# Query-stationary scores, block-diagonal values, a first norm from a channel-major copy of x, and new banks and orders on all engines

## The reference

```python
def _tc_rmsnorm(x, t, gw, gb, bw, bb):
    g = (t @ gw.T + gb)[:, None, :]
    b = (t @ bw.T + bb)[:, None, :]
    inv_rms = jax.lax.rsqrt(jnp.mean(x * x, axis=-1, keepdims=True) + EPS)
    return g * x * inv_rms + b
...
    q, k, v = ((x @ W.T).reshape(B, L, H, dh) for W in (Wq, Wk, Wv))   # 16 heads of 16
    p = jax.nn.softmax(jnp.einsum('blhd,bmhd->bhlm', q, k) / scale, axis=-1)
    o = jnp.einsum('bhlm,bmhd->blhd', p, v).reshape(B, L, D)
    return o @ Wo.T
...
def _swiglu(x, gate_w, hid_w, out_w):
    return jax.nn.silu(x @ gate_w.T) * (x @ hid_w.T) @ out_w.T
x1 = x + _attention(_tc_rmsnorm(x, t, g1w, g1b, b1w, b1b), Wq, Wk, Wv, Wo)
return x + x1 + _swiglu(_tc_rmsnorm(x1, t, g2w, g2b, b2w, b2b), gate_w, hid_w, out_w)
```

## Time and profile before

| | |
|---|---|
| time, median of 3 runs | 991.04 us (990.25 to 996.09) |
| span of the profiled execution | 991.4 us |
| PE / DVE / ACT / POOL busy | 96% / 67% / 57% / 45% |
| share of PE in the chain that ended last | 90% |
| mean granted clock of PE | 0.983 |
| a steady tile, first scores to first scores | about 58.3 us |

### The profile page before, as it was taken

The page is one execution under the profiler, slowest core; times in us unless marked ns, Lnnn a source line. Parts: engine busy times, 40 slices in busy tenths (PEclk is TensorE's granted clock), DMA queues, the critical chain, the costliest instruction groups (busy, mean ns, idle before and its releaser), DMA issues.

```text
span 991.4 us, 24429 instructions
## 1 busy us (share of the span) xinstructions
PE 954.4 (96%) x9112; PEld 817.3 (82%) x9112; DVE 661.2 (67%) x1178; ACT 561.7 (57%) x1271; POOL 447.6 (45%) x393
## 2 busy tenths in 40 slices
PE   6679999999999999999999999999999999999788
PEld 5568888889888898888889888888978888897767
DVE  3856777676777757676675767667576776757552
ACT  6645556565655655565465566646556565655342
POOL 4355345254534535454453545435354552535242
PEclk9688999999999999999999999999999999999999
DMA  5100010000100000010000101000010100000000
GB/s 183 45 1 22 2 38 8 22 21 0 42 0 22 20 21 21 0 42 0 21 21 5 37 0 42 0 21 21 0 42 0 42 0 21 21 0 22 2 22 22
DMA packets 18971, 21.71 MB, mean 22 GB/s; under 512 B 640, under 2 KB 18240, under 8 KB 18816
## 3 DMA queue, kind: packets, MB, share of 16 engines
q1 hardware_dynamic: 18720, 21.24, 6.4%
q10 hardware_dynamic: 224, 0.10, 0.1%
HBM read 12.95 MB, written 8.39 MB: 22 GB/s over the span
## 4 chain that ended last, share of the span: by engine, by line
PE 90%; DVE 3%; ACT 2%; POOL 2%; issue 2%; DMA 1%; DVEq 0%; POOLq 0%; ACTq 0%
PE ps L1051 10%; PE ps L1053 9%; PE ps L1052 9%; PE ps L1143 7%; PE ps L1200 6%; PE ps L1184 6%; PE ps L1151 6%; PE ps L1203 5%; PE ps L1201 5%; PE ps L1192 5%; PE ps L1185 5%; PE ps L1173 3%; PE ps L1077 3%; PE ps L1080 3%; PE ps L1078 3%; PE ps L1069 2%
## 5 line engine op out<-in xcount | busy, mean ns | idle before, releaser
L264 POOL TENSOR_TENSOR h_lo<-h,h_hi 128x512 fp32r<-128x512 f32 x128 | 165.3, 1291 | 251.8 <-ACT h_hi L462 251.8
L270 POOL TENSOR_TENSOR probs<-probs,recip 128x512 f32<-128x512 f32 x128 | 132.8, 1047 | 48.0 <-DVE recip L776 47.8
L1051 PE MATMUL ps<-out_w_hi,h_hi 128*128 128x256 f32 x512 | 150.1, 293 | 0.9
L1053 PE MATMUL ps<-out_w_hi,h_lo 128*128 128x256 f32 x512 | 144.6, 282 | 0.0
L1052 PE MATMUL ps<-out_w_lo,h_hi 128*128 128x256 f32 x512 | 144.2, 282 | 0.0
L799 DVE SCALAR_TENSOR_TENSOR shared<-shared,ps 128x512 f32<-128x512 f32 x128 | 87.4, 683 | 74.9 <-ACT shared L457 74.3
L457 ACT ACTIVATE shared<-ps 128x512 f32<-128x512 f32 x128 | 76.8, 600 | 100.0 <-PE ps L1192 96.4
L1184 PE MATMUL ps<-xn_hi,gate_w_hi 128*128 128x512 f32 x256 | 108.9, 425 | 1.2 <-ACT xn_hi L431 0.8
L1200 PE MATMUL ps<-xn_hi,hid_w_hi 128*128 128x512 f32 x256 | 106.1, 414 | 0.1
L1051 PEld LDWEIGHTS ps<-out_w_hi,h_hi 128*128 128x128 f32 x512 | 96.6, 189 | 11.7 <-POOL h_lo L264 7.3
L472 ACT COPY probsT<-ps 128x512 f32<-128x512 f32 x128 | 73.7, 589 | 56.1 <-PE ps L1151 55.5
(11 more groups left out here) (92 smaller groups left out, 2152.6 us busy)
## 6 DMA issues: line engine op xcount, KB each, us to landing
x_in<-in_x SPq DMA_DIRECT2D x16, 512.0 KB, 3.4
out<-result SPq DMA_DIRECT2D x15, 512.0 KB, 3.0
shared<-in_attT SPq DMA_DIRECT2D x1, 1024.0 KB, 6.8
shared<-in_gateT SPq DMA_DIRECT2D x1, 1024.0 KB, 8.7
shared<-in_hidT SPq DMA_DIRECT2D x1, 1024.0 KB, 4.8
shared<-in_outT SPq DMA_DIRECT2D x1, 1024.0 KB, 6.8
out<-result SPq DMA_DIRECT2D x2, 256.0 KB, 2.2
result<-in_modT SPq DMA_DIRECT2D x1, 256.0 KB, 4.8
```

Of the source, the lines that this page charges most:

```text
L264: nc.gpsimd.tensor_tensor(h_lo[:, j % KEPT, :], h[:, j % 2, :], h_hi[:, j % KEPT, :].bitcast(F32), ALU.subtract).then_inc(h_lo_done, 1)
L270: nc.gpsimd.tensor_tensor(own, own, recip[:, p % TOGETHER, :].unsqueeze(2).to_broadcast([P, SEQS, L]), ALU.mult).then_inc(divided, 1)
L1051: nc.tensor.matmul(dst, a_hi, b_hi, start=first, stop=False, skip_group_check=skip)
L1053: return nc.tensor.matmul(dst, a_lo, b_hi, start=False, stop=last, skip_group_check=skip)
```

## The change

The diff is cut to what moves work; helper functions not shown keep their content.

```diff
+        xT_in = sb("xT_in", [P, CH, TOK])
+        inv1_rows = nc.dram_tensor("inv1_rows", (BLK, P), F32, kind="Internal").ap()
+        inv1_all = sb("inv1_all", [P, TOK])
...
-        queries = sb("queries", [P, CH, SEQS, 2, L])
-        keys = sb("keys", [P, CH, TOK])
-        values = sb("values", [P, BLK, D])
+        queries = sb("queries", [P, CH, TOK])
+        keys = sb("keys", [P, CH, SEQS, 2, L])
+        values = sb("values", [P, SEQS, PAIRS, ROWS])
...
+        def q_bank(u, c):
+            return HIDDEN if alone(u) else PAIR + 3 * c
         def k_bank(u, c):
-            return (GATE, Y)[c] if alone(u) else PAIR + c
+            return (GATE, Y)[c] if alone(u) else PAIR + 1 - c
+        def att_bank(t, r):
+            return PAIR + 2 if r else PAIR if alone(t) else HIDDEN
...
+                if ahead:
+                    sp.wait_ge(scaled1, t + 1)
+                    sp.dma_start(xT_in[:, :, :], xT[t + 1]).then_inc(xT_loaded, 16)
...
+                    sp.wait_ge(inv1_done, t + 2)
+                    sp.dma_start(inv1_rows.rearrange("k p -> p k"), inv1[:, :],
+                                 allow_slow_non_contiguous=True).then_inc(inv1_out, 16)
+                    sp.wait_ge(inv1_out, 16 * t + 16)
+                    sp.dma_start(inv1_all[:, :], inv1_rows.rearrange("k p -> (k p)").unsqueeze(0).to_broadcast([P, TOK])
+                                 ).then_inc(inv1_in, 16)
...
-                for k in range(BLK):
-                    last = nc.vector.tensor_scalar(dst[:, k, :], src[:, k, :], inv[:, k:k + 1], None, ALU.mult)
-                last.then_inc(scaled, 1)
+                nc.vector.tensor_tensor(xn1[:, :, :], xT_in[:, :, :], factors.unsqueeze(1).to_broadcast([P, CH, TOK]),
+                                        ALU.mult).then_inc(scaled1, 1)
...
-                act.wait_ge(v_mm, 2 * u + 1)
+                act.wait_ge(v_mm, 2 * u + 2)
                 wait(act, pv_mm, ROUNDS * u)
-                nc.scalar.copy(values[:, 0:2, :], ps[:, v_bank(u, 0), :].rearrange("p (k n) -> p k n", k=2)
-                               ).then_inc(v_act_done, 1)
+                for head in range(2):
+                    last = nc.scalar.copy(value_rows(0, head), values_of(u, 0, head))
+                last.then_inc(v_act_done, 1)
...
-            def first_heads(t, r):
-            def second_heads(t, r):
...
-                    last = nc.vector.tensor_tensor(
-                        attT_lo[:, r, :].rearrange(by_seq, s=2, q=L)[:, seq, :, :],
+                nc.vector.tensor_tensor(attT_lo[:, r, :], ps[:, att_bank(t, r), :], attT_hi[:, r, :].bitcast(F32),
+                                        ALU.subtract).then_inc(attT_lo_done, 1)
...
-                        last = nc.tensor.matmul(ps[:, bank_of(t, TOGETHER * r + g), tok],
-                                                queries[rows, r, b, :, :].rearrange("p h q -> p (h q)"),
-                                                keys[rows, r, tok], start=True, stop=True)
+                        last = nc.tensor.matmul(ps[seq * L:(seq + 1) * L, bank_of(t, TOGETHER * r + g),
+                                                   k * P:(k + 1) * P],
+                                                queries[rows, r, b * L:(b + 1) * L],
+                                                keys[rows, r, b, :, :].rearrange("p h q -> p (h q)"),
+                                                start=True, stop=True)
...
-                            last = nc.tensor.matmul(ps[g * ROWS:(g + 1) * ROWS, PAIR + 2 * r + seq, tok],
-                                                    values[rows, k, chans], probsT[rows, g, tok],
-                                                    start=True, stop=True)
+                        last = nc.tensor.matmul(ps[g * ROWS:(g + 1) * ROWS, att_bank(t, r), tok],
+                                                values[:, b, TOGETHER * r + g, :], probsT[:, g, tok],
+                                                start=True, stop=True)
...
-                    last = nc.tensor.transpose(ps[:, PAIR + 2 + c, k * P:(k + 1) * P],
+                    last = nc.tensor.transpose(ps[:, GATE + c, k * P:(k + 1) * P],
                                                x_scaled2[:, k, c * P:(c + 1) * P], ident)
...
             def hid(u, j, attend=True):
                 wait(pe, h_done, CHUNKS * u + j)
+                if j == 5 and attend:
+                    pe.wait_ge(attT_lo_done, ROUNDS * (u + 1) + 1)
```

More of the change, by code:

```diff
@@ L379, in _ @@
+            def iteration(t, attend, mlp, finish, ahead):
+                if not mlp and attend:
+                    first_tile(t, ahead)
+                elif not attend and mlp:
+                    after_last(t, finish)
+                elif not attend:
+                    pass
+                elif ahead:
+                    steady_tile(t, finish, ahead)
+                else:
+                    last_tile(t, finish, ahead)
             over_tiles(pool, iteration)
@@ L751, in second_values @@
                 wait(dve, pv_mm, ROUNDS * u)
-                nc.vector.tensor_copy(values[:, 2:4, :], ps[:, v_bank(u, 1), :].rearrange("p (k n) -> p k n", k=2)
-                                      ).then_inc(v_dve_done, 1)
+                if alone(u):
+                    dve.wait_ge(zeros_set, 1)
+                for head in range(2):
+                    last = nc.vector.tensor_copy(value_rows(1, head), values_of(u, 1, head))
+                last.then_inc(v_dve_done, 1)
             def row_maxima(t, p):
@@ L925, in last_tile @@
-                hidden(t - 1, 4)
-                second_heads(t, 0)
-                silu(t - 1, 5)
+                row_maxima(t, 3)
+                silu(u, 1)
+                reciprocals(t, 1)
+                hidden(u, 1)
+                shift(t, 2)
+                shift(t, 3)
+                silu(u, 2)
+                reciprocals(t, 2)
+                hidden(u, 2)
+                reciprocals(t, 3)
+                silu(u, 3)
+                results(t - 2)
+                hidden(u, 3)
@@ new lines, in after_last @@
+            def after_last(t, finish):
+                u = t - 1
+                low_norm2(u)
+                results(t - 2)
+                silu(u, 0)
+                hidden(u, 0)
+                silu(u, 1)
+                hidden(u, 1)
+                silu(u, 2)
+                hidden(u, 2)
+                silu(u, 3)
+                hidden(u, 3)
+                silu(u, 4)
+                hidden(u, 4)
+                silu(u, 5)
+                hidden(u, 5)
+                silu(u, 6)
+                hidden(u, 6)
+                silu(u, 7)
+                hidden(u, 7)
@@ L1235, in _ @@
             pe.wait_ge(consts_in, 16)
-            for c in range(CH):
-                transpose_norm1(0, c, PAIR + c)
+            spread_factors()
             gains_and_shifts(1)
@@ L1336, in last_tile @@
-                down(u, 5)
-                for c in range(CH):
-                    transpose_norm2(t, c)
+                gate(u, 6)
+                hid(u, 6)
+                project_q(t + 1, 0)
+                transpose_probs(t, 7)
+                project_k(t + 1, 0)
+                values_probs(t, 1)
+                project_q(t + 1, 1)
+                gate(u, 7)
+                project_out(t, ahead)
+                hid(u, 7)
+                project_k(t + 1, 1)
+                down(u, 5)
@@ L1434, in iteration @@
-                if attend:
-                    for c in range(CH):
-                        transpose_norm2(t, c)
-                if mlp:
-                    down(u, 6)
-                    down(u, 7)
+                if not mlp and attend:
+                    first_tile(t, ahead)
+                elif not attend and mlp:
+                    after_last(t, finish)
+                elif not attend:
+                    pass
+                elif ahead:
+                    steady_tile(t, finish, ahead)
+                else:
+                    last_tile(t, finish, ahead)
```

1087 lines of the change are left out of this document (498 added, 589 removed).

## The result

The changed kernel takes 1065.99 us (median of 4 runs, 1061.75 to 1070.37) against 992.12 of the kernel before. The ratio is 1.0742, with a 95% interval of 1.072 to 1.0764: slower, where 967 us and faster had been forecast. The profiled execution has a span of 1063.4 us, so 72.0 us are to be explained against the span of 991.4 before.

The account below looks back on a forecast made before the run. PE, busy 96% of the span, was taken to bound the 14 steady tiles, chains through other engines both ends. 991.4 - 15.5 (steady tiles) - 1 (tile 0) - 7 (tile 15, last MLP) = 967.9, stated as 967; range 948 to 988.

Parts of the forecast that it names:

- the way of 1/rms through DRAM is hidden: Steady tile: 1/rms ready at about 17.5, needed at 27.1; two transfers take about 6 us of 9.6, so no cost.
- rival C: 1/rms trip through DRAM: DVE waits at its product, paying any excess over 9.6 us in 14 tiles; chance 0.07.
- PE's work in a steady tile: Eight transposes gone -0.85, scores calls 1.94 to 1.2 (-1.5), values calls 1.09 to 1.3 (+0.4): -1.9 us per tile.
- A: Rival on scores calls: only four places overlap, 2.8 us instead of 1.2, +51 over 32 calls, 1018 us; chance 0.07.
- B: Rival on values calls: the four column strips do not overlap, 3.4 us instead of 1.3, +67, 1034 us; chance 0.04.
- rule on row groups: Values calls: weight loads overlap running products only when row groups differ, so a call would be nearer 3.4 than 1.3 us.
- The stall for the value copies: Steady tile's end: PE's scores wait for ACT's two value copies behind the second norm's casts, 0.5 us.
- The second stall: First norm: DVE's 128x1024 product (1.2 us) makes xn1 late for PE's query projection, 0.3 us taken, bounds 0.2 to 1.4.
- The steady tile: Tiles 1 to 14: -1.9 work + 0.5 + 0.3 stalls = -1.1 us each, to 57.2 us; -15.5 us over 14 tiles.
- Tile 15 and the last MLP: End of kernel: -6 in tile 15, -1 in the last MLP, together -7 us (bounds -12 and 0).
- the stall of about 3 us for hidden 4: Tile 15: round 0's values call writes HIDDEN and waits for hidden 4 behind some eight DVE operations, about 3 us.
- Tile 0: First tile: output projection starts at about 60.5 against 61.9, the new values wait takes most back: -1 us (bounds -5, +3).

Follow-up runs that it names:

- the row written once: Changed kernel with the write of 1/rms to DRAM made in tile 0 alone, the read kept in every tile: 975.07 us, span 973.0.
- 16-byte version: Changed kernel with the DRAM row laid out token by token, written as 128 pieces of 16 bytes, DVE reading with a stride of four: 985.81 us.
- the best version: Changed kernel with 16-byte pieces, ACT copying the row into token order, POOL's tile 0 first-norm remainder ahead of both weight remainders, value copies unmoved: 972.96 us.

## Why the prediction was wrong

**The step that failed** is "the way of 1/rms through DRAM is hidden", in two ways: its length was mis-sized, and the sum has no term for what the write does to engines that do not wait for it. Its size: about 6 us were put down for the whole way, because the first transfer has 512 pieces like x's load. The pieces of that load are 1 KB; the count carried over and the place of the pieces did not. The write alone took 10.7 us in the tile shown, and DVE's product started 503.65 - 489.54 = 14.1 us after its issue. The two ends of the slack were right: the write is issued 17.7 us after the tile's first scores (forecast 17.5), and with the row written once DVE reaches its product at 26.8 (27.1). With the pieces 64 bytes apart the row lands about 5 us after the write's issue, and the way is hidden as forecast. Its price: prediction and rival C both took the transfer for something that costs only whoever waits for its result. C got the way's length right (over 11.3 us) and the reason wrong in the same manner: DVE's waits for the row are 36.6 us in all, while PE's gaps and the slower clock behind them, 84.5 us, fall on engines that do not read the row. A way of 14.1 us by C's own rule gives 967 + 14 x (14.1 - 9.6) = 1030; the write on its own, in the kernel before, where nothing near it waits for it, already costs 32 us.

**The rule that fed C.** The Trainium skill, DMA: Bandwidth & Descriptors, Specifications, says that below 512 bytes the DMA does a read-modify-write. The runs limit that: 4-byte pieces, 64 bytes apart, land with 1.4 us of waiting and cost nothing, so a piece far under 512 bytes is not dear by itself; sixteen of them in the same 64 bytes cost 8.9. The runs do not show how the DMA makes such a write. The warning pointed at the right transfer, and I let it change a chance only, since no row of the kernel before had such a write: the bound from above that an unseen transfer needs was missing from the sum.

**What was right.** With the write out of the way the remaining terms can be read off. PE's work in a steady tile: scores 1.14 (forecast 1.2), values 1.03 (1.3, and below the 1.09 that had been called a lower bound), eight transposes gone; A and B fall. For B that sets the Trainium skill's rule on row groups (TensorE: Matmul & The Clock Gate, Part 3, The mechanism) against a second row: 64 products on four column strips that share all rows take 1.03 us, 16 ns each, where 3.4 us had been worked out for no overlap, so their loads do overlap. The stall for the value copies: 0.85, forecast 0.5, because the copies end at +5.82 instead of +5.65 (489.46 + 1.19 - 484.83), and the scores start 0.35 behind them where 0.1 was put down. The second stall: the product takes 1.23 (forecast 1.2), but at the query projection PE hardly waits for POOL's low part (about 0.1 us in a steady tile); elsewhere PE waits 0.4 for DVE's activation product at a gate (5.5 us in 14 waits), and that this is near the forecast 0.3 is luck. The steady tile: 56.9, forecast 57.2. That is in part luck too: the work fell by 2.6 us where 1.9 was forecast (2 x 0.80 for scores, 2 x 0.06 for values, 0.85), and the two stalls take 1.25 back instead of 0.8. Tile 15 and the last MLP: 91.4 against 99.5, -8.1, forecast -7; the stall of about 3 us for hidden 4 is there (3.2, once).

**Tile 0** was wrong on its own: forecast -1, measured +9.8 with the row written once (82.58 against 72.79) and +12.5 in the changed kernel. The prediction said that POOL's weight remainder stands ahead of the first norm's low part, and priced that as a small loss; PE's wait there is 7.7 us (4.9 before). The stall for the values, 3.5 us, was not in the sum at that size, and neither were the waits for the softmax at PE's transposes. Putting POOL's remainder first took the 7.7 to 3.8. And about half of the +9.8 stands ahead of tile 0's first scores, which start at 26.10 instead of 21.13: the forecast has no term for the start. There PE's first product starts 1.9 us later (7.98 against 6.08), behind the load of the modulation, ahead of which SP now issues xT's; and at its first projection PE waits 3.55 us for DVE's low part of the first norm, where it had no wait before.

So without the packed write the change comes near the forecast of 967 (a span of 973.0): the 14 steady tiles gain 20.1 us where 15.5 was forecast, and tile 0 with its start loses 9.8 where a gain of 1 was. With the write it is slower than before, because one new transfer was costed by its nearest row and not from both sides.

## What to carry to other kernels

A new transfer has to be priced by where its pieces land, not only by count and bytes: many 4-byte pieces into the same 64 bytes of DRAM held up engines that had nothing to do with them, while as many pieces 64 bytes apart, or a quarter as many 16 bytes wide, held up none. Time marked issue on an engine whose code has no wait there is a reason to look at what SP issued some microseconds earlier, and at whether another run names a releaser at the same place. And a stall in a chain of four engines is worth only what the next one in line leaves over; two orders of one tile end are compared by its length, not by the wait that one of them removes.

## What the runs showed of the hardware that was not expected

A packed write of 2 KB holds engines while the trace shows no packet in flight. Why they are held is open. In the changed kernel PE is held in 13 of the 14 tiles after tile 0. It stops 3.2 to 7.6 us after the write's issue, at an instruction that differs from tile to tile (values, a gate, a down chunk) though the code is the same; where it is the values call, it stops between two of its 64 products. It goes on for good 7.6 to 11.2 us after the issue, close to the landing. ACT is held in 5 of the 14, for 3.8 to 5.9 us. POOL's idle times called issue (56.4 us in 14 tiles) are none of it: with 16-byte pieces POOL stands the same 4.0 us at the same place, there for DVE's reciprocal. In the kernel before, with the same write, it is ACT in 6 tiles, DVE in one of them and PE in none.

The trace goes one step further for ACT. In all 11 of its gaps in these two kernels the bracket says remote, and the semaphore that it waits for is one of PE's; the trace has that update 3.1 to 7.4 us after the end of the PE product that makes it, and ACT starts within 0.3 us of it. In the kernels without the packed write, or with it in tile 0 alone, no update of PE comes more than 0.4 us late. So by the trace ACT waits for a signal that is late, and not for instructions of its own, of which the trace records no transfer between 200 and 920 us, where most of the gaps are. For PE's own stops between two products no signal is known, and their cause stays open.

The trace also loses records in these stretches: of the 2947 semaphore updates that the compute engines' instructions make, the changed kernel's trace lacks 114, the kernel before with the packed write lacks 33 of 3041, and the kernels with no packed write, or with one in tile 0 alone, lack none. The update by DVE's reciprocal is among the missing in all 14 tiles of the changed kernel, which is why POOL's wait for it is called issue. The writing of the trace itself is therefore caught in the hold, and may have a part in it: no run here tells whether the engines would be held as long without a trace.

In most tiles one of POOL's 128x512 divisions runs beside DVE's 128x1024 product. By line (count; least/median/most ns), with DVE's product at 2.04 us (16-byte version, strided) and at 1.23 us (the best version):

```profile
L290 POOL TENSOR_TENSOR probs<-probs,recip x128: 1039/1046/2969, 33.9 to 926.0; 128x512 f32<-128x512 f32 x128
```

```profile
L292 POOL TENSOR_TENSOR probs<-probs,recip x128: 1040/1045/2133, 34.3 to 913.3; 128x512 f32<-128x512 f32 x128
```

The longest division is the median plus about the length of DVE's product (1.05 + 2.04 = 3.1 against 2.97, and 1.05 + 1.23 = 2.3 against 2.13), so POOL seems to stand while the product runs. In the changed kernel, where no division meets the product, the longest takes 1.53. That is probably how a longer DVE operation made PE wait for POOL's divisions: 14.7 us in 19 waits in the 16-byte version, 5.9 in 6 in the best.
